# One of eight drive products of a selective scan moved from VectorE to GpSimd, and two TensorE steps put ahead of a sum

## The chip, the cores and the metric

The kernel is one program on one core of a Trainium2 chip. The metric is the device time of one execution in microseconds; three runs of the kernel before give a median of 766.16 us (764.79 to 766.89). PE is TensorE, DVE VectorE, ACT ScalarE, POOL GpSimd and SP SyncE.

## What is computed

A small fusion model runs over 16 sequences of 113 tokens (36 image patches and 77 text tokens) with 256 channels: patch embedding, attention, a mixture of experts, then a state-space layer and a quantised feed-forward layer. The change lies in the state-space layer. Cut to what matters, for one sequence:

```python
delta = softplus(rank @ dt_proj_w.T + dt_proj_b)             # token x channel
dA  = exp(delta[..., None] * A)                              # 16 states
dBu = delta[..., None] * Bp[:, :, None, :] * xc[..., None]
ys  = scan(h[t] = dA[t] * h[t-1] + dBu[t])
y   = (ys * Cp[:, :, None, :]).sum(-1) + xc * D_param
y   = y * silu(res)
return y @ out_proj_w.T + out_proj_b + (x @ skip_proj_w.T + skip_proj_b)
```

`Bp` and `Cp` depend on token and state, not on the channel. `delta * xc` (called `dx` in the kernel) depends on token and channel, not on the state. So the drive `dBu` of one state is `dx` times one row of B.

## The kernel before

Channels lie on the partitions (2 blocks of 128), tokens along the free axis. The 16 sequences make 8 groups of two, N = 226 tokens each. The 16 states make 8 chunks of two, so a tile of a chunk is 128 x 904: two states, two channel blocks, 226 tokens. Every engine runs its own program over groups and chunks, written out by hand (`step` in `pool_ssm`, `act_ssm`, `dve_ssm` and `pe_ssm`), and they meet by semaphores; groups 1 to 4 run in a hardware loop, two to a turn, the others are written out. Within a chunk c of a group g:

- PE, `spread` (L1832 to 1842): two products with a selection matrix copy the two rows of B to all 128 partitions, into PSUM bank 2 or 3 by the parity of c. It is issued one chunk ahead, at the head of PE's chunk c - 1, and waits until the drive that read the bank last is done.
- DVE, `drives` (L1327 to 1333): `dx` times the spread B from PSUM, into one of two drive buffers. One product of 128 x 904.
- ACT, `decays` (L821 to 829): exp(delta A) of each state into PSUM, one chunk ahead, each of the two after the scan that read that buffer last.
- DVE, `scans` (L1335 to 1342): two scans of 128 x 452, state = decay * state + drive.
- POOL (L501 to 522): `read`, the product of the states with C (128 x 904), after both scans of the chunk. In chunks 0, 1, 2, 3 and 7 (`PAIRED`) POOL then adds the two states, a pair sum of 128 x 452.
- PE, `reduce` (L1844 to 1862): adds `read`, or the pair sum, to the sum over the states in PSUM. It is issued in PE's next chunk, behind the spread.

Other work is put between these at fixed chunks, by constants. On DVE in chunk 1 `gate` (L1344), the product with silu(res) of the group before, and in chunk 2 `add_resid` (L1349), the residual and its statistics. On ACT the silus in chunk 1, `projections` (L796) in chunk 3, softplus in chunk 4. On POOL, at the head of chunk 3 `without_high` (L486), which waits for ACT's projections of the next group, of chunk 5 the two step products `steps` (L494), of chunk 6 `without_mid`. On PE, in the order of `step` (L1879): chunk 3 issues spread, reduce of chunk 2, `project_dt`, then the first half of `skip` (the skip projection of this group, L1864); chunk 4 issues spread, reduce of chunk 3, the second half of `skip`, and `turn`, which transposes the normalised rows of the group after the next; chunks 5 and 6 issue the two halves of `project_in` behind the reduce. Group 6 has no `turn` and no `project_in`, and in group 7 DVE also does the next layer's layernorm: statistics behind the scans of chunk 3, rows behind those of chunks 4 to 7.

The ordering of POOL's and DVE's chunks, in the kernel's own words:

```python
# pool_ssm.step, chunk c
pool.wait_ge(state_ready, 2 * k + 4)        # both scans of this chunk
pool.wait_ge(read_used, k + 1)
pool.tensor_tensor(read[kp], state[kp], c_all[...], ALU.mult)
if c in PAIRED:
    pool.tensor_tensor(read[kp][:, 0], read[kp][:, 0], read[kp][:, 1], ALU.add)
# dve_ssm.step, chunk c
drives(g, c, par)
if before and c == AT_GATE: gate(g - 1, 1 - par)
scans(g, c)
if before and c == AT_RESID: add_resid(g - 1)
```

Of the kernel before, what the change touches and what calls it, by code (L numbers as in the profile page):

```python
# [17 lines left out]
P = 128  # L18
# [38 lines left out]
AT_NORMALISE, AT_TURN, AT_COPY, AT_IN, AT_PAD, AT_CONV = 0, 4, 5, 5, 6, 7  # L57
OPENING = 1
AT_SKIP = (3, 4)
FILL = (19, 2, 4)  # L60
# [51 lines left out]
def build(nc, a, out):  # L112
    ctx = ExitStack()
    with ctx:
# [3 lines left out]
        def sem(name):  # L118
            return ctx.enter_context(nc.semaphore(name))
# [18 lines left out]
        work = sb("work", [P, WORK])  # L138
        ident = const[:, C_ID:C_ID + P]

        def psb(bank):
# [148 lines left out]
        read = [pl.take((2, KT, N)) for _ in range(2)]  # L290
        yT = pl.take((KT, N))


# [57 lines left out]
        xn2_ready, xn2T_ps, xT2_ready = sem("xn2_ready"), sem("xn2T_ps"), sem("xT2_ready")  # L351
        logitsT_ps, logitsT_ready = sem("logitsT_ps"), sem("logitsT_ready")
        logits_ps, route, chosen_ready, counts_ps, slots_ready = (sem("logits_ps"), sem("route"), sem("chosen_ready"),
# [15 lines left out]
        yT_ready, ssm_ps, resid3_ready = sem("yT_ready"), sem("ssm_ps"), sem("resid3_ready")  # L369
        pair_ready, decay_zero, shift_ready = sem("pair_ready"), sem("decay_zero"), sem("shift_ready")  # L370
        patch_in = [sem(f"patch_in{n}") for n in range(PK // 2)]
# [111 lines left out]
        def pool_ssm(pool):  # L483
# [10 lines left out]
            def steps(g, par):  # L494
# [4 lines left out]
                pool.tensor_tensor(dx[par], delta[par], xc[par], ALU.mult).then_inc(dx_ready, 1)  # L499

            def step(g, par, c_loads, more=True):  # L501
                for c in range(CHUNKS):
                    k = g * CHUNKS + c
                    kp = c % 2
                    if more and c == AT_REST:
                        without_high(g + 1)
                    if more and c == AT_STEPS:
                        steps(g + 1, 1 - par)
                    if more and c == AT_LOW:
                        pool.wait_ge(read_ready, k + 2)  # L510
                        without_mid(g + 1, 1 - par)
                        pool.wait_ge(bc3_ready, g + 2)
                    if c == 0:
                        pool.wait_ge(c_in[par], c_loads)
                    pool.wait_ge(state_ready, 2 * k + 4)
                    pool.wait_ge(read_used, k + 1)
                    pool.tensor_tensor(read[kp], state[kp], c_all[par][:, 2 * c:2 * c + 2, :].unsqueeze(2).broadcast_to([P, 2, KT, N]), ALU.mult)\  # L517
                        .then_inc(read_ready, 1)
                    if c in PAIRED:
                        pool.wait_ge(read_ready, k + 3)  # L520
                        pool.tensor_tensor(read[kp][:, 0], read[kp][:, 0], read[kp][:, 1], ALU.add).then_inc(pair_ready, 1)  # L521
# [127 lines left out]
        def act_shared(act):  # L649
            def gate(n, par):  # L650
                act.wait_ge(sgate_ps, n + par + 1)
                act.wait_ge(sh_ready, n + par + 1)
                act.activation(s_gate[:, par, :], ps[:, 3 + 2 * par, 0:4 * S], ACT.Silu).then_inc(sgate_ready, 1)  # L653

            for par in range(2):
                gate(0, par)
            act.wait_ge(logitsT_ps, 1)
            act.activation(logitsT, ps[:, 7, 0:4 * S], ACT.Copy).then_inc(logitsT_ready, 1)
            with act.Fori(1, (4 * HT) // 2) as i:
                for par in range(2):  # L660
                    gate(2 * i, par)
# [99 lines left out]
        def act_ssm(act):  # L761
# [47 lines left out]
            def softplus(g):  # L809
# [9 lines left out]
                act.activation(sp_abs, sp_abs, ACT.Ln, bias=1.0).then_inc(softplus_ready, 1)  # L819

            def decays(g, c, par, first=False):  # L821
                k = g * CHUNKS + c
# [8 lines left out]
            def step(g, par, more=True, before=True, turn_next=True):  # L831
                for c in range(CHUNKS):
# [9 lines left out]
                    if c < CHUNKS - 1:  # L842
                        decays(g, c + 1, par)
                    elif more:
                        decays(g + 1, 0, 1 - par)
                    if not before and c == OPENING:
                        pad(1)
# [20 lines left out]
            decays(0, 0, 0, first=True)  # L868
            act.wait_ge(shift_ready, 1)
            step(0, 0, before=False)  # L870
# [158 lines left out]
        def dve_router(dve):  # L1029

            dve.wait_ge(logits_ps, 1)
            q = Seq(dve, route)
# [263 lines left out]
        def dve_ssm(dve):  # L1296
# [11 lines left out]

            for counted in (state_ready, read_ready, read_used, drive_ready):
                dve.sem_inc(counted, 2)  # L1310
# [24 lines left out]
            def scans(g, c):  # L1335
                k, kp = g * CHUNKS + c, c % 2
                dve.wait_ge(drive_ready, k + 3)
                dve.wait_ge(read_ready, k + 1)
# [18 lines left out]
            def step(g, par, more=True, before=True, turn_next=True):  # L1357
                for c in range(CHUNKS):
                    drives(g, c, par)
                    if before and c == AT_GATE:  # L1360
# [18 lines left out]
            normalise(1)  # L1379
            dve.scalar_tensor_tensor(out=shift[:, :], in0=mean[:, :], scalar=-1.0, in1=rstd[:, :], op0=ALU.mult, op1=ALU.mult).then_inc(shift_ready, 1)  # L1380
            dve.wait_ge(wqT_ready, 2 + 2 * FT + FT // 2)
            for n in range(2):
                dve.memset(decay_ps(n)[:, :, 0:1], 0.0).then_inc(decay_zero, 1)
            dve.wait_ge(decay_zero, 2)
            opening_steps()
# [174 lines left out]
        def pe_scores(pe):  # L1560

            pe.wait_ge(xT2_ready, B)
            for k in range(KT):
                for g in range(4):
                    rows = slice(ROUTED * g, ROUTED * g + ROUTED)
                    last = pe.matmul(ps[rows, 7, 0:4 * S], router_w[:, k, :], xT2[:, k, g * 4 * S:(g + 1) * 4 * S], start=k == 0,
                                     stop=k == KT - 1, tile_position=(0, ROUTED * g), skip_group_check=True)
            last.then_inc(logitsT_ps, 1)

# [212 lines left out]
        def pe_ssm(pe):  # L1782
# [49 lines left out]

            def spread(g, c, par):

                k, kp = g * CHUNKS + c, c % 2
                if c == 0:
                    pe.wait_ge(bc3_ready, g + 1)
                    pe.wait_ge(proj_ready, 4 * g + 4)
                pe.wait_ge(drive_ready, k + 1)
                for n in range(2):  # L1840
# [38 lines left out]
            def step(g, par, more=True, before=True, turn_next=True):  # L1879
                for c in range(CHUNKS):  # L1880
                    if c < CHUNKS - 1:
                        spread(g, c + 1, par)
                    elif more:
                        spread(g + 1, 0, 1 - par)
# [8 lines left out]
                    if before and c == AT_OUT:  # L1893
                        project_out(g - 1)
                    if c > 0:
                        reduce(g, c - 1, par)
                    if more and c == AT_RANK:
                        project_x(g + 1, 1 - par)
                    if more and c == AT_DT:
                        project_dt(g + 1)  # L1900
                    if c in AT_SKIP:
                        if before:
                            pe.wait_ge(resid3_ready, g)
                        skip(g, par, AT_SKIP.index(c))
                    if turn_next:
                        if c == AT_TURN:
                            turn(g + 2)
                        if AT_IN <= c < AT_IN + 2:
                            project_in(g + 2, par, c - AT_IN)
                        if c == AT_CONV:  # L1910
                            convolve(g + 2, (0,))
# [15 lines left out]
            turn(1)  # L1927
            spread(0, 0, 0)
            step(0, 0, before=False)
# [106 lines left out]
```

## Time and profile before

| | |
|---|---|
| median of 3 runs | 766.16 us (764.79 to 766.89) |
| profiled execution | 768.96 us |
| its span, first to last instruction | 767.0 us |
| granted TensorE clock, mean | 0.965 of full speed |
| scan stage (first drive to last gate) | about 440 to 693 us |

The times of rows of the trace are counted from the start of the span. The chip's answer to a wait is read from the row behind it: in square brackets stands how long the engine idled before the row, and the line that released it.

### The profile page before, as it was taken

The page shows a single profiled execution, that of the slowest core. Times are in us where ns is not written, and L with a number is a line of the kernel's source. Part 1 is how long each engine was busy: PE and PEld are TensorE (multiplying, and loading weights), DVE is VectorE, ACT ScalarE, POOL GpSimd, SP SyncE. Part 2 cuts the span into 40 slices and gives each one's busy share as a digit, 9 for nine tenths or more (in the row PEclk, how much of TensorE's full clock was granted, in tenths as well). Part 3 has the DMA queues.
Part 4 walks back from the last instruction along what each step waited for, and adds up shares of the span by engine and source line. Part 5 has one row for each costly group of instructions (what it writes and reads, how often), then busy time and mean ns, then how long its engine had stood idle before and what let it go on. Part 6 is the DMA issues. An engine that isn't in the chain of part 4 may idle for free. (4 is left out here: it accounts for less than half of the span.)

```text
span 767.0 us, 11714 instructions
## 1 busy us (share of the span) xinstructions
PE 689.1 (90%) x3814; PEld 453.1 (59%) x3814; DVE 493.9 (64%) x895; ACT 375.6 (49%) x852; POOL 296.3 (39%) x249
## 2 busy tenths in 40 slices
PE   7789999998999999999996689899899897759986
PEld 5568888886566655666664556557566564324444
DVE  1466666666542215444215779998999899995686
ACT  0366666665311122233222666875876774212964
POOL 0011111110026013111211058888888888430436
PEclk9999999999999999999998899999999999978999
DMA  9990000001213041111004202202201201000003
GB/s 242 359 409 23 0 0 0 0 0 38 88 26 98 0 120 35 49 42 35 21 28 112 98 14 84 99 14 85 97 25 72 98 33 66 0 0 1 1 0 97
DMA packets 17831, 50.04 MB, mean 65 GB/s; under 512 B 3935, under 2 KB 12291, under 8 KB 15619
## 3 DMA queue, kind: packets, MB, share of 16 engines
q1 hardware_dynamic: 15683, 43.79, 16.6%
q0 software_dynamic: 2112, 5.77, 2.7%
q8 instruction: 22, 0.36, 0.2%
q14 instruction: 14, 0.11, 0.0%
HBM read 42.85 MB, written 6.70 MB: 65 GB/s over the span
## 5 line engine op out<-in xcount | busy, mean ns | idle before, releaser
L517 POOL TENSOR_TENSOR arena<-arena 128x904 f32<-128x904 f32 x64 | 125.0, 1953 | 43.6 <-DVE arena L1341 39.5
L1341 DVE TENSOR_TENSOR_SCAN arena<-ps,arena 128x452 f32<-128x452 f32 x128 | 133.6, 1086 | 6.9 <-ACT ps L828 2.1
L828 ACT ACTIVATE ps<-arena,sh_w 128x448 f32<-128x448 f32 x128 | 79.1, 631 | 71.8 <-DVE arena L1341 71.5
L1666 PE MATMUL ps<-arena,work 128*128 x176 | 84.2, 603 | 0.0
L592 ACT ACTIVATE work<-ps,work 113x113 f32<-113x113 f32 x256 | 66.8, 387 | 31.3 <-DVE work L960 31.3
L1331 DVE TENSOR_TENSOR arena<-arena,ps 128x904 f32<-128x904 f32 x64 | 69.2, 1081 | 11.6 <-PE ps L1841 11.3
L563 POOL DMA_INDIRECT answers_e<-work,slot_token x22 | 21.6, 980 | 135.1 <-DVE work L1131 132.3
L456 POOL TENSOR_TENSOR xT<-work 128x452 f32<-128x452 f32 x16 | 15.1, 943 | 141.2 <-DVE work L949 141.2
L1854 PE MATMUL ps<-arena,const 128*128 128x452 f32 x80 | 42.5, 615 | 19.1 <-POOL arena L521 18.7
L1859 PE MATMUL ps<-arena,const 128*128 128x452 f32 x96 | 44.7, 590 | 12.5 <-POOL arena L517 12.5
L1127 DVE TENSOR_TENSOR work<-ps,work 128x512 f32<-128x512 f32 x22 | 15.2, 692 | 55.8 <-PE ps L1666 50.1
L1615 PE MATMUL ps<-xT,sh_w 128*128 128x452 f32 x128 | 50.3, 545 | 0.0
L521 POOL TENSOR_TENSOR arena<-arena 128x452 f32<-128x452 f32 x40 | 45.7, 1143 | 3.1
L1678 PE MATMUL ps<-arena,work 128*128 x176 | 42.5, 384 | 3.5 <-ACT work L674 3.5
L1666 PEld LDWEIGHTS ps<-arena,work 128*128 128x128 f32 x176 | 31.5, 194 | 23.2 <-issue 22.6
L960 DVE TENSOR_REDUCE work<-ps 113x4 f32<-113x452 f32 x64 | 35.7, 621 | 10.6 <-PE ps L1469 10.6
L1678 PEld LDWEIGHTS ps<-arena,work 128*128 128x128 f32 x176 | 32.0, 192 | 7.9 <-issue 4.4
L1615 PEld LDWEIGHTS ps<-xT,sh_w 128*128 128x128 f32 x128 | 23.8, 190 | 21.7 <-issue 20.8
L653 ACT ACTIVATE work<-ps 128x452 f32<-128x452 f32 x16 | 8.7, 548 | 55.3 <-PE ps L1615 55.3
L1448 PE MATMUL ps<-work 128*128 128x113 f32 x256 | 33.2, 284 | 2.4 <-ACT work L586 1.7
L670 ACT ACTIVATE work<-ps 128x512 f32<-128x512 f32 x22 | 13.2, 598 | 45.0 <-PE ps L1666 45.0
L1475 PE MATMUL ps<-const,work 113*113 113x113 f32 x256 | 33.6, 264 | 1.7 <-ACT work L592 1.7
(270 smaller groups left out, 1385.5 us busy)
## 6 DMA issues: line engine op xcount, KB each, us to landing
arena<-c_rows SPq DMA_DIRECT2D x8, 1808.0 KB, 6.4
arena<-in_ex_w SPq DMA_DIRECT2D x8, 1536.0 KB, 21.6
rows_in<-xn SPq DMA_DIRECT2D x4, 448.0 KB
xn<-answers_e SPq DMA_DIRECT2D x4, 448.0 KB
out<-resid SPq DMA_DIRECT2D x8, 224.0 KB
arena<-in_patches SPq DMA_DIRECT2D x3, 576.0 KB, 6.3
sh_w<-in_sh_w SPq DMA_DIRECT2D x1, 1536.0 KB, 12.8
resid<-in_txt SPq DMA_DIRECT2D x1, 1232.0 KB
```

Source lines behind the costliest of these rows:

```text
L517: pool.tensor_tensor(read[kp], state[kp], c_all[par][:, 2 * c:2 * c + 2, :].unsqueeze(2).broadcast_to([P, 2, KT, N]), ALU.mult)\
L521: pool.tensor_tensor(read[kp][:, 0], read[kp][:, 0], read[kp][:, 1], ALU.add).then_inc(pair_ready, 1)
L592: last = act.activation(probs[:, r, j], ps[0:S, 3 + r, j * S:(j + 1) * S], ACT.Exp, bias=negmax[:, h:h + 1])
L828: act.activation(decay_ps(n)[:, :, 1:], delta[par].rearrange("p k (b s) -> p (k b) s", b=GB)[:, :, 1:], ACT.Exp, scale=a_neg[:, 2 * c + n: ...
L960: dve.tensor_reduce(negmax[:, 4 * r:4 * r + 4].unsqueeze(2), ps[0:S, 3 + r, 0:4 * S].rearrange("p (j s) -> p j s", j=4), AX.X, ALU.max, ne ...
L1331: dve.tensor_tensor(drive[kp], dx[par].unsqueeze(1).broadcast_to([P, 2, KT, N]), ps[:, 2 + kp, 0:2 * N].rearrange("p (n s) -> p n s", n=2) ...
L1341: dve.tensor_tensor_scan(state[kp][:, n].rearrange("p k s -> p (k s)"), decay_ps(n).rearrange("p q s -> p (q s)"), drive[kp][:, n].rearran ...
L1615: last = pe.matmul(ps[:, bank, 0:4 * S], sh_w[:, at + k * HID + m * P:at + k * HID + (m + 1) * P], xT2[:, k, bass.ds(g * 4 * S, 4 * S)], s ...
L1666: last = pe.matmul(ps[:, bank, :], xgT[par][:, k, :], arena[:, bass.ds(e * EW + at + k * HID, HID)], start=k == 0, stop=k == KT - 1)
L1678: last = pe.matmul(ps[:, 6, 0:D], e_hT[:, m, :], arena[:, bass.ds(e * EW + DOWN + m * D, D)], start=m == 0, stop=m == HT - 1)
L1854: pe.matmul(ps[:, 6, 0:KT * N], ident, read[kp][:, 0].rearrange("p k s -> p (k s)"), start=False, stop=c == CHUNKS - 1, skip_group_check=T ...
L1859: last = pe.matmul(ps[:, 6, 0:KT * N], ident, read[kp][:, n].rearrange("p k s -> p (k s)"), start=False, stop=False, skip_group_check=True)
```

## The change

In chunk 3 of every group, DVE makes no drive. ACT copies the spread B of that chunk from PSUM to a new tile of 128 x 452 in SBUF, `b_copy`, behind the decays of chunk 3. POOL multiplies `dx` by that copy into the drive buffer, at the head of its chunk 3: behind the product with C and the pair sum of chunk 2, ahead of `without_high`. DVE's scans of chunk 3 wait for that product, and so does PE's spread of chunk 5, which reuses the bank. On PE, the second half of `skip` and `turn`, both in chunk 4, are issued ahead of the reduce of chunk 3 instead of behind it. To have semaphores for this, some elsewhere are shared now: the router's two products use one (`logits_ps`), the zeroing of the decays and the shift of the layernorm another (`entry_ready`); `drive_ready` counts seven drives a group. The core of the diff:

```diff
+POOL_DRIVE = 3
+DVE_DRIVES = CHUNKS - 1
...
+        def dve_drives(g, c):
+            return DVE_DRIVES * g + c + 1 - (c > POOL_DRIVE)
...
+        b_copy = pl.take((2, N))
...
+            def drives(g, c, par):
+                k, kp = g * CHUNKS + c, c % 2
+                pool.wait_ge(b_copied, g + 1)
+                pool.wait_ge(dx_ready, g + 1)
+                pool.tensor_tensor(drive[kp], dx[par].unsqueeze(1).broadcast_to([P, 2, KT, N]),
+                                   b_copy.unsqueeze(2).broadcast_to([P, 2, KT, N]), ALU.mult).then_inc(pool_drive_ready, 1)
+
             def step(g, par, c_loads, more=True):
                 for c in range(CHUNKS):
                     k = g * CHUNKS + c
                     kp = c % 2
+                    if c == POOL_DRIVE:
+                        drives(g, c, par)
                     if more and c == AT_REST:
                         without_high(g + 1)
...
+            def copy_b(g, c):
+                act.wait_ge(b_ps, g * CHUNKS + c + 1)
+                if not isinstance(g, int) or g > 0:
+                    act.wait_ge(pool_drive_ready, g)
+                act.activation(b_copy, ps[:, 2 + c % 2, 0:2 * N].rearrange("p (n s) -> p n s", n=2), ACT.Copy).then_inc(b_copied, 1)
...
                         decays(g, c + 1, par)
                     elif more:
                         decays(g + 1, 0, 1 - par)
+                    if c + 1 == POOL_DRIVE:
+                        copy_b(g, c + 1)
...
-                dve.wait_ge(drive_ready, k + 3)
+                if c == POOL_DRIVE:
+                    dve.wait_ge(pool_drive_ready, g + 1)
+                else:
+                    dve.wait_ge(drive_ready, dve_drives(g, c))
...
-                    drives(g, c, par)
+                    if c != POOL_DRIVE:
+                        drives(g, c, par)
...
-                pe.wait_ge(drive_ready, k + 1)
+                if c == POOL_DRIVE + 2:
+                    pe.wait_ge(pool_drive_ready, g + 1)
+                elif c >= 2:
+                    pe.wait_ge(drive_ready, dve_drives(g, c - 2))
+                elif not first:
+                    pe.wait_ge(drive_ready, dve_drives(g - 1, CHUNKS + c - 2))
...
+                    if c == AT_SKIP[1]:
+                        skip(g, par, 1)
+                    if turn_next and c == AT_TURN:
+                        turn(g + 2)
                     if c > 0:
                         reduce(g, c - 1, par)
...
-                    if c in AT_SKIP:
+                    if c == AT_SKIP[0]:
                         if before:
                             pe.wait_ge(resid3_ready, g)
-                        skip(g, par, AT_SKIP.index(c))
+                        skip(g, par, 0)
                     if turn_next:
-                        if c == AT_TURN:
-                            turn(g + 2)
```

## Rows read from the trace of the kernel before

**Rows 1.** The page's costliest groups: count, busy us, mean ns, idle before and its releaser

```profile
L517 POOL TENSOR_TENSOR arena<-arena 128x904 f32<-128x904 f32 x64 | 125.0, 1953 | 43.6 <-DVE arena L1341 39.5
L1341 DVE TENSOR_TENSOR_SCAN arena<-ps,arena 128x452 f32<-128x452 f32 x128 | 133.6, 1086 | 6.9 <-ACT ps L828 2.1
```

**Rows 2.** Two of five stretches from gate to gate: us, then PE, PEld, DVE, ACT, POOL

```profile
504.02:533.53 29.51, 27.28 (x109) 17.84 (x108) 26.76 (x30) 20.93 (x41) 24.80 (x18) 0.94 0.17 64
533.53:561.77 28.24, 25.95 (x111) 17.22 (x110) 26.51 (x28) 20.48 (x40) 24.32 (x18) 1.00 0.16 66
```

**Rows 3.** Timeline of group 3, all engines: start us, us, row, idle before it

```profile
537.27 2.09 DVE L1341 TENSOR_TENSOR_SCAN arena<-ps,arena 128x452 f32<-128x452 f32 x2
...
539.43 1.96 POOL L517 TENSOR_TENSOR arena<-arena 128x904 f32<-128x904 f32 x1
...
540.75 1.08 DVE L1331 TENSOR_TENSOR arena<-arena,ps 128x904 f32<-128x904 f32 x1
540.92 1.19 ACT L828 ACTIVATE ps<-arena,sh_w 128x448 f32<-128x448 f32 x2
541.47 1.15 POOL L521 TENSOR_TENSOR arena<-arena 128x452 f32<-128x452 f32 x1
541.97 2.09 DVE L1341 TENSOR_TENSOR_SCAN arena<-ps,arena 128x452 f32<-128x452 f32 x2
...
542.52 0.45 ACT L800 ACTIVATE arena<-ps,sh_w 64x226 f32<-64x226 f32 x1 [0.41 <-PE ps L1823]
...
543.98 1.07 DVE L1331 TENSOR_TENSOR arena<-arena,ps 128x904 f32<-128x904 f32 x1
...
544.57 1.94 POOL L517 TENSOR_TENSOR arena<-arena 128x904 f32<-128x904 f32 x1
...
547.79 1.03 PE L1854 MATMUL ps<-arena,const 128*128 128x452 f32 x2 [0.85 <-POOL arena L521]
...
550.10 0.55 ACT L764 ACTIVATE arena<-ps 128x452 f32<-128x452 f32 x1 [0.57 <-PE ps L1793]
...
551.92 1.94 POOL L517 TENSOR_TENSOR arena<-arena 128x904 f32<-128x904 f32 x1
...
557.55 1.10 DVE L1331 TENSOR_TENSOR arena<-arena,ps 128x904 f32<-128x904 f32 x1 [0.66 <-PE ps L1841]
```

**Rows 4.** Timeline of DVE: three rows of group 2, the stall of group 6

```profile
507.76 2.09 DVE L1341 TENSOR_TENSOR_SCAN arena<-ps,arena 128x452 f32<-128x452 f32 x2
...
522.48 1.10 DVE L1331 TENSOR_TENSOR arena<-arena,ps 128x904 f32<-128x904 f32 x1 [1.51 <-PE ps L1841]
...
529.09 1.10 DVE L1331 TENSOR_TENSOR arena<-arena,ps 128x904 f32<-128x904 f32 x1
...
633.59 1.10 DVE L1331 TENSOR_TENSOR arena<-arena,ps 128x904 f32<-128x904 f32 x1 [1.13 <-PE ps L1841]
```

**Rows 5.** Timeline of PE, group 2, chunk 4: the sum and the skip product

```profile
518.29 1.55 PE L1854 MATMUL ps<-arena,const 128*128 128x452 f32 x2 [0.86 <-POOL arena L521]
519.63 1.91 PE L1868 MATMUL ps<-sh_w,arena 128*113 128x256 f32 x4
```

**Rows 6.** Stretches of 2 us, groups 2 and 3: columns as rows 2, then PE's clock

```profile
518.00:520.00 2.00, 1.71 (x3) 0.93 (x4) 1.87 (x3) 1.96 (x5) 2.00 (x2) 0.66 1.08 427
...
546.00:548.00 2.00, 1.15 (x7) 0.69 (x6) 2.00 (x3) 1.94 (x5) 1.92 (x3) 1.00 1.05 405
```

**Rows 7.** Timeline of group 0, chunk 3: decays, scans, product with C

```profile
455.38 1.19 ACT L828 ACTIVATE ps<-arena,sh_w 128x448 f32<-128x448 f32 x2
...
456.15 2.09 DVE L1341 TENSOR_TENSOR_SCAN arena<-ps,arena 128x452 f32<-128x452 f32 x2 [2.06 <-ACT ps L828]
...
458.56 1.95 POOL L517 TENSOR_TENSOR arena<-arena 128x904 f32<-128x904 f32 x1
```

**Rows 8.** Timeline of DVE in group 7: scans of chunks 2 and 3

```profile
651.03 2.09 DVE L1341 TENSOR_TENSOR_SCAN arena<-ps,arena 128x452 f32<-128x452 f32 x2
...
655.52 2.09 DVE L1341 TENSOR_TENSOR_SCAN arena<-ps,arena 128x452 f32<-128x452 f32 x2
```

More of the change, by code:

```diff
@@ L351, in build @@
         xn2_ready, xn2T_ps, xT2_ready = sem("xn2_ready"), sem("xn2T_ps"), sem("xT2_ready")
-        logitsT_ps, logitsT_ready = sem("logitsT_ps"), sem("logitsT_ready")
+        b_copied, logitsT_ready = sem("b_copied"), sem("logitsT_ready")
         logits_ps, route, chosen_ready, counts_ps, slots_ready = (sem("logits_ps"), sem("route"), sem("chosen_ready"),
@@ L369, in build @@
         yT_ready, ssm_ps, resid3_ready = sem("yT_ready"), sem("ssm_ps"), sem("resid3_ready")
-        pair_ready, decay_zero, shift_ready = sem("pair_ready"), sem("decay_zero"), sem("shift_ready")
+        pair_ready, entry_ready, pool_drive_ready = sem("pair_ready"), sem("entry_ready"), sem("pool_drive_ready")
         patch_in = [sem(f"patch_in{n}") for n in range(PK // 2)]
@@ L656, in act_shared @@
                 gate(0, par)
-            act.wait_ge(logitsT_ps, 1)
+            act.wait_ge(logits_ps, 1)
             act.activation(logitsT, ps[:, 7, 0:4 * S], ACT.Copy).then_inc(logitsT_ready, 1)
@@ L868, in act_ssm @@
             decays(0, 0, 0, first=True)
-            act.wait_ge(shift_ready, 1)
+            act.wait_ge(entry_ready, 1)
             step(0, 0, before=False)
@@ L1029, in dve_router @@
         def dve_router(dve):
-            dve.wait_ge(logits_ps, 1)
+            dve.wait_ge(logits_ps, 2)
             q = Seq(dve, route)
@@ L1307, in dve_ssm @@
             dve_layernorm(dve, 3, FIRST_SEQS)
-            for counted in (state_ready, read_ready, read_used, drive_ready):
+            for counted in (state_ready, read_ready, read_used):
                 dve.sem_inc(counted, 2)
@@ L1379, in dve_ssm @@
             normalise(1)
-            dve.scalar_tensor_tensor(out=shift[:, :], in0=mean[:, :], scalar=-1.0, in1=rstd[:, :], op0=ALU.mult, op1=ALU.mult).then_inc(shift_ready, 1)
+            dve.scalar_tensor_tensor(out=shift[:, :], in0=mean[:, :], scalar=-1.0, in1=rstd[:, :], op0=ALU.mult, op1=ALU.mult).then_inc(entry_ready, 1)
             dve.wait_ge(wqT_ready, 2 + 2 * FT + FT // 2)
             for n in range(2):
-                dve.memset(decay_ps(n)[:, :, 0:1], 0.0).then_inc(decay_zero, 1)
-            dve.wait_ge(decay_zero, 2)
+                dve.memset(decay_ps(n)[:, :, 0:1], 0.0).then_inc(entry_ready, 1)
+            dve.wait_ge(entry_ready, 3)
             opening_steps()
@@ L1567, in pe_scores @@
                                      stop=k == KT - 1, tile_position=(0, ROUTED * g), skip_group_check=True)
-            last.then_inc(logitsT_ps, 1)
+            last.then_inc(logits_ps, 1)
         def pe_turn_scores(pe):
@@ L1831, in project_dt, with spread @@
                 last.then_inc(dt_ps, 1)
-            def spread(g, c, par):
+            def spread(g, c, par, first=False):
                 k, kp = g * CHUNKS + c, c % 2
@@ L1881, in step @@
                     if c < CHUNKS - 1:
-                        spread(g, c + 1, par)
+                        spread(g, c + 1, par, not before)
                     elif more:
@@ L1927, in pe_ssm @@
             turn(1)
-            spread(0, 0, 0)
+            spread(0, 0, 0, True)
             step(0, 0, before=False)
```

## The prediction

> **What bounds the kernel now.** I read the page's costliest groups first: POOL's product with C (64 of 1953 ns) and DVE's scans (128 of 1086 ns) lead them [rows 1], and both lie in the scan stage, so shares over the whole span, which has other stages with other limits, say little. The stretches from gate to gate then give one group each: 29.51 us with 26.76 us of DVE and 24.80 us of POOL, then 28.24 us with 26.51 and 24.32 us [rows 2]; three more groups are like these. DVE is all but full, so its work per group looks like the thing to cut, but POOL has less than 4 us free, and each needs the other's result.
>
> The timeline of group 3, where nothing is disturbed, shows the order [rows 3]. Call T the end of the second scan of chunk 2: 537.27 + 2.09 = 539.36. POOL starts the product with C of chunk 2 at 539.43, right at T, and its pair sum at 541.47; both are behind the scans, never ahead of them. DVE spends T to T+1.4 on the residual and its statistics, makes the drive of chunk 3 at 540.75 and starts its scans at 541.97, T+2.6. The next drive follows at 543.98, so a chunk takes DVE 3.23 us. POOL starts its product of chunk 3 at 544.57, T+5.2, and of chunk 5 at 551.92; PE sums that product, projects and spreads, and only then can DVE start the next group's first drive, at 557.55 after 0.66 us of idling: T+18.2. So two chains, DVE's and POOL's into PE's, end within 0.7 us of each other.
>
> Groups 2 and 5 are longer because the drive of chunk 6 waits 1.51 us in both for its spread [rows 4]. PE was waiting for the pair sum of chunk 3, then did the sum in 1.55 us and the skip product behind it in 1.91 us [rows 5]; its granted clock was 0.66 in 518 to 520 us, falling to its lower level (1.2 GHz), while the same stretch of group 3 kept 1.00 (2.4 GHz) [rows 6].
>
> **The change part by part.**
>
> DVE loses one drive a group. Drive to first scan is 1.22 us (540.75 to 541.97) [rows 3]; eight groups give 9.8 us of DVE time back. That is the whole possible gain of this part, and it counts only where DVE isn't then waiting.
>
> ACT gains a copy of 128x452 from PSUM, behind the decays of chunk 3. The nearest row is the copy of the same size, 0.55 us; an upper bound is two of 0.45 us, 0.9 us [rows 3]; I take 0.55. The decays of chunk 3 end at 540.92 + 1.19 = 542.11 [rows 3], so the copy is there at about 542.66, T+3.3. What is queued behind it on ACT are the projections; they started at 542.52 after 0.41 us of waiting [rows 3], so they come some 0.2 us later; POOL's subtraction, which waits for them, stands behind the new product now and loses nothing.
>
> POOL gains a product of 128x904. It isn't in the trace. The product with C has the same shape, 1.95 us; from below, DVE's drive of 1.08 us, from above, two pair sums, each of half the size, at 1.15 us, 2.3 us [rows 3]. I take 1.95, by engine and shape. The Trainium skill (GPSIMD Engine Reference, section 3.1) measures the two-input product on this engine at 1.96 times DVE's; applied to 1.08 us that would be an estimate of 2.1 us and would add 0.15 us to each of eight groups.
>
> Its place matters more than its length. It stands at the head of POOL's chunk 3, behind chunk 2's product with C and pair sum. The pair sum ends at 541.47 + 1.15 = 542.62, T+3.26, the copy at T+3.3; the product runs to T+5.25 and, with 0.07 us to hand over (539.36 to 539.43), chunk 3's scans start at T+5.3 instead of T+2.6 [rows 3]. DVE is done with the residual at T+1.4, and the drive of chunk 4 is written behind those scans, so it idles 3.9 us there, pays 2.7 us for the 1.2 us it saves, and everything behind it moves by 2.7.
>
> From there both chains are followed to the next group's first drive. DVE: scans to T+7.3, then the drives of chunks 4 to 7 and 0, four steps of 3.23 us: T+20.2. POOL: chunk 3's product with C starts at T+7.45 instead of T+5.2, 2.25 us later; from there to chunk 5's product POOL took 7.35 us (544.57 to 551.92) [rows 3] and has the same to do, so that and PE's work behind it move by 2.25: T+20.45. The later one counts: **+2.25 us** an ordinary group, three of them (1, 3, 4). The 0.66 us stall is eaten by the shift.
>
> PE's skip product and turn ahead of the sum: PE has them done while it waits for the pair sum, and the spread of chunk 6 then follows the sum at once. In groups 2 and 5 the 1.51 us goes, but a DVE that arrives 2.7 us later wouldn't have met most of it: those groups reach their first drive at T+20.45 too. Group 2 did so at 529.09, with T = 507.76 + 2.09 = 509.85, T+19.24 [rows 4]: **+1.2 us** each. Alone, the reordering would be worth at most two times 1.51 us. In group 6 there is no in-projection of a coming group; DVE alone sets the pace, and the shift of 2.7 us eats its stall of 1.13 us [rows 4]: **+1.6 us**.
>
> Group 0 and group 7. In group 0 the decays of chunk 3 end at 455.38 + 1.19 = 456.57; with the copy, 457.1, and the product, 459.1, scans start at 459.2 instead of 456.15: 3.0; POOL's product with C starts at 461.35 instead of 458.56: **+2.8** [rows 7]. In group 7, T = 651.03 + 2.09 = 653.12, and scans start at T+5.3 = 658.4 instead of 655.52 [rows 8]: **+2.8**; DVE has layernorm work behind every later chunk there and nothing absorbs it.
>
> The shared semaphores cost nothing: the counts they wait for are reached at the same points as before.
>
> Sum: 3 x 2.25 + 2 x 1.2 + 1.6 + 2.8 + 2.8 = **16.4 us longer** (16.35). The profiled execution took 768.96 us and would take 785.4; the median of the runs is 766.16, 2.8 below it, and with 16.4 it is **782.6 us**.
>
> **The rivals.**
>
> A second loss, PE's clock. PE idles longer before the sum of chunk 3 and before those of 4 and 5. For it: the 0.85 us gap of group 3 and the 0.86 us gap of group 2 look alike, and the clock fell in one [rows 3, 5, 6]. Against it: low stretches sat in chunks 3 to 5, where the new order leaves slack. If the low level reaches the sum of chunk 5, in-projection and spread (551.92 + 1.94 = 553.86 to 557.55, 3.7 us [rows 3]) over half their length, each of the five groups 1 to 5 loses 1.8 us more: 9 us, about 791. The Trainium skill (TensorE: Matmul & The Clock Gate, Part 1) says idling drops the array to half rate; taken for every such gap, that would be this rival. The row of group 3 at 1.00 speaks against taking it for every gap.
>
> The reordering does not do what it says: if the sum itself at the low level, 1.55 us, still holds the spread of chunk 6, groups 2 and 5 keep their 1.5 us behind the new wait: +3 us, 785.6.
>
> The other side, faster: POOL makes the product before DVE asks for it. It decides at T+0.65: started by then, the product of 1.95 us ends by T+2.6, where the scans started before. Then groups 2, 5 lose their stalls, groups 0, 6 and 7 gain about 1.2 us each, and ordinary groups stay, for POOL's chain through chunk 5 sets them: 2 x 1 + 3 x 1.2 = 5.6 us less, 760.5. Against it: the written order puts a product and a pair sum, 3.1 us, between T and the start. Were it only half true, the result would be no change.
>
> **How the numbers follow.** Forecast 0.71, clock 0.14, reordering without effect 0.10, the other side 0.05, of which 0.03 faster and 0.02 within 0.3%, which is about 2.3 us and what a measurement of this kernel can tell from no change. So faster 0.03, same 0.02, slower 0.95. Range: from below, DVE's chain alone (T+20.2) in every ordinary group and 0.3 us less in each of the others, 2.5 us less in all, and a product 0.4 us quicker than its nearest row in eight groups, 3.2 us: 777. From above, the clock rival at 791, which also holds a product of 2.3 us (+2.8). The product at DVE's 1.08 us (0.87 us less, eight times) would take another 3.8 us off, 773, and is left out, as 64 rows of POOL say otherwise.
>
> **What would show it.** Right: DVE idle for some 3.9 us before the scans of chunk 3 in each group, released by a new POOL line of 8 products of about 1.95 us; 56 drives on DVE instead of 64; 8 ACT copies of about 0.55 us; gates 30.3 to 30.7 us apart; no wait of chunk 6's drive for its spread. Wrong: chunk 3's scans starting by T+3, a product well under 1.9 us, or gates still 28 us apart.

## The result, and the profile after

The changed kernel takes 786.16 us (median of 4 runs, 781.77 to 787.52), the kernel before 765.75 us in the same comparison: 1.0259 times as long, with a 95% interval of 1.0222 to 1.0296. The forecast was 782.6 us, with a range of 777 to 791. The profiled execution took 786.44 us, its span 784.5 us.

The costliest groups of the page, columns as in [rows 1], now put a wait in front of the scans that wasn't there. Lines have moved: in the changed kernel L1367 is the scans, L532 POOL's product with C, L536 its pair sum, L511 its new product, L840 ACT's copy, L1354 DVE's drives, L1873 PE's spread, L1886 and L1891 its sums of a pair sum and of a whole product, L1830 the in-projection.

```profile
L1367 DVE TENSOR_TENSOR_SCAN arena<-ps,arena 128x452 f32<-128x452 f32 x128 | 133.6, 1086 | 41.2 <-POOL arena L511 37.2
L532 POOL TENSOR_TENSOR arena<-arena 128x904 f32<-128x904 f32 x64 | 124.9, 1952 | 57.8 <-DVE arena L1367 52.5
...
L1354 DVE TENSOR_TENSOR arena<-arena,ps 128x904 f32<-128x904 f32 x56 | 60.4, 1078 | 6.8 <-PE ps L1873 6.6
```

The scans took 6.9 us of idling before, and 37.2 of the 41.2 us now end with L511, POOL's new product: 3.8 to 4.0 us in each of groups 1 to 7 and 9.5 in group 0, where DVE idled 3.4 us for the spread and 2.1 for the decays before. The instructions that were there take as long as before, a scan 1086 ns and the product with C 1952 (1953 before), so nothing in these rows says that the two engines slow each other. There are 56 drives on DVE instead of 64, as asked for, and POOL in its turn idles longer for the scans (52.5 us instead of 39.5). The view of the new line itself:

```profile
L511 POOL TENSOR_TENSOR arena<-arena x8: 1935/1937/1940, 452.8 to 670.0; 128x904 f32<-128x904 f32 x8
```

Least, median and greatest duration are the same to 5 ns: 1.94 us against the 1.95 forecast. Its place, in the timeline of group 3 (T, the end of chunk 2's second scan, is 542.53 + 2.09 = 544.62), beside [rows 3]:

```profile
542.53 2.09 DVE L1367 TENSOR_TENSOR_SCAN arena<-ps,arena 128x452 f32<-128x452 f32 x2
...
544.70 1.95 POOL L532 TENSOR_TENSOR arena<-arena 128x904 f32<-128x904 f32 x1
...
546.72 1.14 POOL L536 TENSOR_TENSOR arena<-arena 128x452 f32<-128x452 f32 x1
547.31 0.53 ACT L840 ACTIVATE arena<-ps 128x452 f32<-128x452 f32 x1
...
547.91 1.94 POOL L511 TENSOR_TENSOR arena<-arena 128x904 f32<-128x904 f32 x1
...
550.08 2.09 DVE L1367 TENSOR_TENSOR_SCAN arena<-ps,arena 128x452 f32<-128x452 f32 x2 [3.98 <-POOL arena L511]
...
552.25 1.94 POOL L532 TENSOR_TENSOR arena<-arena 128x904 f32<-128x904 f32 x1 [1.86 <-DVE arena L1367]
...
565.33 1.10 DVE L1354 TENSOR_TENSOR arena<-arena,ps 128x904 f32<-128x904 f32 x1 [0.33 <-PE ps L1873]
```

POOL's product with C, pair sum and new product stand one behind the other, ACT's copy ends at 547.84, just as the pair sum does (547.86), and DVE starts chunk 3 at T+5.46 after 3.98 us of idling. The next group's first drive comes at T+20.71. The forecast had T+5.3, 3.9 us and T+20.45.

By stretch, columns as in [rows 2], with PE's granted clock behind POOL's; the first runs from the first drive to the gate in group 1, the others from gate to gate:

```profile
435.85:475.02 39.17, 33.97 (x128) 23.21 (x127) 28.02 (x28) 23.79 (x46) 27.30 (x19) 0.88 0.15 61
475.02:508.04 33.02, 29.05 (x110) 18.74 (x109) 25.71 (x27) 21.59 (x42) 26.60 (x19) 0.90 0.15 58
508.04:538.79 30.75, 27.89 (x110) 18.07 (x109) 25.52 (x27) 21.20 (x41) 26.32 (x19) 0.94 0.16 61
538.79:569.55 30.76, 27.82 (x109) 18.02 (x109) 25.52 (x29) 21.41 (x41) 26.54 (x19) 0.94 0.15 61
569.55:600.25 30.70, 27.76 (x109) 18.00 (x108) 25.61 (x28) 21.55 (x41) 26.68 (x19) 0.94 0.16 61
600.25:630.69 30.44, 27.81 (x111) 18.11 (x110) 25.62 (x29) 20.89 (x40) 26.46 (x19) 0.94 0.16 62
630.69:661.10 30.41, 22.86 (x81) 12.32 (x80) 25.51 (x28) 19.08 (x35) 26.36 (x19) 0.94 0.17 62
661.10:709.04 47.94, 31.93 (x105) 14.44 (x104) 40.51 (x63) 8.63 (x15) 22.69 (x14) 0.88 0.00 0
```

Against the same stretches of the kernel before (first drive at 440.15, gates from 475.78 to 693.01) the scan stage is 273.19 instead of 252.86 us, 20.3 us longer. The span grew by 17.5 only: this execution reached its first drive 4.3 us earlier, and took 1.5 us longer behind the last gate. The profiles of the kernels below, which do the same work up to there, reach it between 435.4 and 439.7 us, and take 73.6 to 75.5 us behind the last gate (74.0 before), so neither is part of the change. DVE's work in a group fell by 1.0 us, and the group grew by 2.5.

Group 1, at 33.02 us, is longer than the rest. PE and DVE there:

```profile
491.69 1.03 PE L1886 MATMUL ps<-arena,const 128*128 128x452 f32 x2 [2.03 <-POOL arena L536]
...
493.68 3.38 PE L1891 MATMUL ps<-arena,const 128*128 128x452 f32 x4 [0.77 <-POOL arena L532]
496.85 3.17 PE L1830 MATMUL ps<-arena,sh_w 128*128 128x226 f32 x8
499.86 0.36 PE L1873 MATMUL ps<-arena,xT 96*128 96x226 bf16 x2
...
500.26 1.10 DVE L1354 TENSOR_TENSOR arena<-arena,ps 128x904 f32<-128x904 f32 x1 [2.25 <-PE ps L1873]
```

PE had its skip product and turn done and idled 2.03 us for the pair sum of chunk 3. Then the sum of chunk 4 took 3.38 us and the in-projection 3.17, where they take 1.79 and 1.69 in group 2, and chunk 7's drive waited 2.25 us for the spread behind them. The clock of the stretch, columns as in [rows 6]:

```profile
494.00:496.00 2.00, 2.00 (x3) 0.85 (x3) 1.87 (x3) 1.42 (x3) 1.92 (x3) 0.50 0.01 4
```

0.50 is the lower of the two levels, 1.2 GHz.

### The profile page after: what moved, and what is told of

It reads as the page before. It is cut to its first block and busy times, and to the rows that moved or that the text cites. A ratio compares the mean times of both kernels' runs of the same rounds, so it can differ in the third digit from the quotient of the medians.

```text
span 784.5 us, 11763 instructions
## 1 busy us (share of the span) xinstructions
PE 699.3 (89%) x3814; PEld 458.2 (58%) x3814; DVE 485.9 (62%) x887; ACT 380.8 (49%) x860; POOL 311.0 (40%) x257
## 5 line engine op out<-in xcount | busy, mean ns | idle before, releaser
L1367 DVE TENSOR_TENSOR_SCAN arena<-ps,arena 128x452 f32<-128x452 f32 x128 | 133.6, 1086 | 41.2 <-POOL arena L511 37.2
L532 POOL TENSOR_TENSOR arena<-arena 128x904 f32<-128x904 f32 x64 | 124.9, 1952 | 57.8 <-DVE arena L1367 52.5
L1693 PE MATMUL ps<-arena,work 128*128 x176 | 83.1, 596 | 0.0
L1891 PE MATMUL ps<-arena,const 128*128 128x452 f32 x96 | 49.8, 647 | 20.8 <-POOL arena L532 20.8
L1354 DVE TENSOR_TENSOR arena<-arena,ps 128x904 f32<-128x904 f32 x56 | 60.4, 1078 | 6.8 <-PE ps L1873 6.6
L1886 PE MATMUL ps<-arena,const 128*128 128x452 f32 x80 | 40.4, 587 | 19.4 <-POOL arena L536 18.8
L536 POOL TENSOR_TENSOR arena<-arena 128x452 f32<-128x452 f32 x40 | 45.7, 1143 | 3.1
L1705 PE MATMUL ps<-arena,work 128*128 x176 | 41.8, 380 | 3.4 <-ACT work L689 3.4
L1891 PEld LDWEIGHTS ps<-arena,const 128*128 128x128 f32 x96 | 18.7, 216 | 36.3 <-POOL arena L532 24.9
L1705 PEld LDWEIGHTS ps<-arena,work 128*128 128x128 f32 x176 | 31.8, 190 | 7.8 <-issue 4.4
```

Of the source, the lines that this page charges most:

```text
L1354: dve.tensor_tensor(drive[kp], dx[par].unsqueeze(1).broadcast_to([P, 2, KT, N]), ps[:, 2 + kp, 0:2 * N].rearrange("p (n s) -> p n s", n=2) ...
L1367: dve.tensor_tensor_scan(state[kp][:, n].rearrange("p k s -> p (k s)"), decay_ps(n).rearrange("p q s -> p (q s)"), drive[kp][:, n].rearran ...
L1693: last = pe.matmul(ps[:, bank, :], xgT[par][:, k, :], arena[:, bass.ds(e * EW + at + k * HID, HID)], start=k == 0, stop=k == KT - 1)
L1705: last = pe.matmul(ps[:, 6, 0:D], e_hT[:, m, :], arena[:, bass.ds(e * EW + DOWN + m * D, D)], start=m == 0, stop=m == HT - 1)
L1886: pe.matmul(ps[:, 6, 0:KT * N], ident, read[kp][:, 0].rearrange("p k s -> p (k s)"), start=False, stop=c == CHUNKS - 1, skip_group_check=T ...
L1891: last = pe.matmul(ps[:, 6, 0:KT * N], ident, read[kp][:, n].rearrange("p k s -> p (k s)"), start=False, stop=False, skip_group_check=True)
```

## The experiments

Times are medians; a ratio is to runs of the kernel before on the same chip (766.42, 765.44 and 766.10 us in the three comparisons), with its 95% interval. Stage is the time from the first drive to the last gate in the profiled execution: 252.86 us before, 273.19 us changed.

### The reordering alone

```diff
+                    if c == AT_SKIP[1]:
+                        skip(g, par, 1)
+                    if turn_next and c == AT_TURN:
+                        turn(g + 2)
                     if c > 0:
                         reduce(g, c - 1, par)
```

(in the kernel before; the same calls are taken out behind the sum)

> The kernel before with the reordering alone: PE issues the skip product's second half and the turn ahead of the sum of chunk 3; DVE still makes all eight drives. My theory: the reordering takes out the two waits of 1.51 us of chunk 6's drive (groups 2 and 5), and nothing else, so some 2 to 3 us under the kernel before: 763 to 764, with no wait of chunk 6's drive left in the trace. Rival (the reordering does nothing, since the clock falls all the same and the sum holds the spread): within 1 us of the kernel before, the 1.5 us waits still there. Rival (the reordering itself costs part of the loss of the change): slower than before by over 2.3 us.

762.84 us, 0.9966 times (0.9950 to 0.9982); stage 250.39. Groups 1 to 4 take 28.23, 28.24, 28.23 and 28.22 us, group 5 28.09, so the two of 29.5 and 29.1 us are gone, and with them the waits of 1.51 us. Group 2, columns as above:

```profile
500.69:528.93 28.24, 25.77 (x110) 16.97 (x109) 26.50 (x29) 20.68 (x40) 24.57 (x18) 1.00 0.17 67
```

The theory holds, and this kernel is faster than both, though only by 0.3% than the kernel before.

### The move alone

The changed kernel with those lines where they were before.

> The changed kernel with PE's order of before: only the drive of chunk 3 is moved to POOL. My theory: the move is the whole loss, 4 us of DVE waiting a group; the reordering matters less behind it than by itself. 786 to 789, DVE idle for 3.9 to 4.0 us before the scans of chunk 3 in each group. Rival (the reordering is part of the loss): under 784.

797.81 us, 1.0401 times (1.0377 to 1.0425); stage 281.51. The theory held for the wait (3.98 to 4.11 us in groups 1 to 7, 9.5 in group 0 as in the changed kernel) and missed the size, 9 us above its band: without the reordering the stage is 8.3 us longer than the changed kernel's (5.6 longer than in its second profile below), not up to 3. Group 1 shows why:

```profile
495.64 1.87 PE L1886 MATMUL ps<-arena,const 128*128 128x452 f32 x2 [3.29 <-POOL arena L536]
497.30 1.91 PE L1900 MATMUL ps<-sh_w,arena 128*113 128x256 f32 x4
```

PE now idles 3.29 us for the pair sum, then runs at the lower level (0.50 in 496 to 500 us) through the sum and the skip product, and chunk 6's spread stands behind both: DVE's drive waits 1.63 us for it. What happened to two groups in the kernel before now happens to all five that have a turn (31.8 to 33.0 us).

### Chunk 3 without a drive

Copy, product and their waits are taken out of the changed kernel; nothing replaces them.

> Nobody makes the drive of chunk 3: ACT's copy and POOL's product are left out, and the scans of chunk 3 read the drive buffer as chunk 1 left it, with no wait for POOL; PE's order is that of the change. It shows what DVE's time would have been worth at best. My theory: POOL's chain through chunk 5 into PE's spread sets the ordinary groups anyway, so of 9.8 us of DVE time only some 3 to 6 come through, with the 2 to 3 of the reordering: 757 to 763. Rival (DVE alone is the bound): the full 9.8 and the reordering, 753 to 755. Rival (the loss isn't in the wait, but in something else the change brings, such as the shared semaphores or code): 770 or more.

762.48 us, 0.9950 times (0.9934 to 0.9966); stage 248.46. At the upper end of the theory's band. Beside the reordering alone, DVE has eight drives less to make, and the groups are as long as there, for instance group 2:

```profile
501.90:530.17 28.27, 25.78 (x110) 16.97 (x109) 25.62 (x28) 20.70 (x40) 24.59 (x18) 1.00 0.18 67
```

28.27 us, with 25.62 us of DVE work instead of 26.50. Only group 7 is 2.0 us shorter. So of the 9.8 us of DVE time about 2 us come through: the best that the change could have given, had the product cost nothing. This kernel keeps the shared semaphores, so they are not the loss either.

### The product with nobody waiting for it

```diff
-                pool.tensor_tensor(drive[kp], dx[par]...
+                pool.tensor_tensor(unread, dx[par]...
```

(DVE doesn't wait for it; PE's spread of chunk 5 waits for the copy)

> As the kernel without a drive of chunk 3, but ACT makes the copy and POOL the product, at the place and of the size of the change; the product goes to a tile that nobody reads, and nobody waits for it but the copy's next turn (the scans of chunk 3 read the buffer as chunk 1 left it). It keeps the load on POOL and ACT and takes away DVE's wait. My theory: the load lies mostly in POOL's idle time ahead of chunk 3's product with C, and shifts that by some 0.6 us a group; 759 to 766, and the 20 us of the loss are the wait. Rival (POOL's load is the loss, 8 products of 1.95 us): 775 to 780.

767.86 us, 1.0019 times (1.0003 to 1.0036); stage 254.92. The theory's band ended at 766, so the load costs a little more than I held, 6.5 us of stage against no product at all, some 0.5 us an ordinary group (28.24 to 28.27 becomes 28.73 to 28.80) and 2.9 in group 7. Group 2:

```profile
500.78:529.54 28.76, 26.02 (x110) 16.99 (x109) 25.72 (x28) 21.12 (x41) 26.42 (x19) 1.00 0.17 66
```

The other 18.3 us (273.19 less 254.92) are DVE's wait and what follows from it, PE's clock included; against the kernel below in which the clock holds (269.34) they are 14.4.

### The product ahead of the pair sum

```diff
                         .then_inc(read_ready, 1)
+                    if c + 1 == POOL_DRIVE:
+                        drives(g, c + 1, par)
                     if c in PAIRED:
```

(and taken out at the head of chunk 3)

> The changed kernel with POOL's product one place earlier: behind the product with C of chunk 2, but ahead of its pair sum (1.1 us). Theory A: POOL's queue alone holds the product; it then starts at T+2.1 and DVE's wait shrinks from 4.0 to 2.9 us: 7 groups by 1.1, some 778 to 780 (less what the later pair sum takes back). Theory B, mine: ACT's copy comes at T+3.2 too, behind the silus and the decays of chunk 3, so the product can't start earlier; DVE's wait stays 3.9 to 4.0 us, POOL idles 1.1 us for the copy, and the pair sum comes 3 us later, which PE's sum and all behind it in chunk 3 pay: 786 to 792.

808.93 us, 1.0574 times (1.0542 to 1.0606). Theory B's steps are all there in group 1 (T = 482.84 + 2.09 = 484.93):

```profile
485.01 1.94 POOL L530 TENSOR_TENSOR arena<-arena 128x904 f32<-128x904 f32 x1
...
487.63 0.53 ACT L840 ACTIVATE arena<-ps 128x452 f32<-128x452 f32 x1
...
488.23 1.93 POOL L511 TENSOR_TENSOR arena<-arena 128x904 f32<-128x904 f32 x1 [1.27 <-ACT arena L840]
...
490.12 1.14 POOL L536 TENSOR_TENSOR arena<-arena 128x452 f32<-128x452 f32 x1
490.39 2.09 DVE L1367 TENSOR_TENSOR_SCAN arena<-ps,arena 128x452 f32<-128x452 f32 x2 [3.96 <-POOL arena L511]
...
491.31 1.87 PE L1886 MATMUL ps<-arena,const 128*128 128x452 f32 x2 [3.14 <-POOL arena L536]
...
499.35 1.10 DVE L1354 TENSOR_TENSOR arena<-arena,ps 128x904 f32<-128x904 f32 x1 [3.66 <-PE ps L1873]
```

The product can't start before the copy, DVE waits as long as ever, and the pair sum of chunk 2 comes 3 us late. What I had too small is what that costs: PE idles 3.14 us for it, does the sum, `project_dt` and the skip product at the lower level (0.50 from 492 to 501 us), and DVE waits another 3.66 us for the spread of chunk 5 behind them. Groups of 34.5 us, and 17 us above the top of the band.

### Chunk 4's drive instead, one place ahead

`POOL_DRIVE = 4`; ACT's copy stands behind the decays of chunk 3, POOL's product at the head of its chunk 3.

> The same move for chunk 4 instead of chunk 3, one place ahead: ACT copies the spread of chunk 4 behind the decays of chunk 3, POOL makes the product at the head of its chunk 3, ahead of the scans of chunk 3, DVE asks for it only behind those. Same load on every engine as in the changed kernel. My theory (the place is the loss, not the load): the product runs at T+4 to T+6, DVE asks for it at T+4.7 and waits some 1.3 us instead of 4.0; POOL's product with C of chunk 3 starts about 1.2 us late, so 766 to 774. Rival (the load of the product and the copy is the loss): within 4 us of the changed kernel, 782 to 790.

771.41 us, 1.0083 times (1.0054 to 1.0111); stage 257.46. Inside the theory's band, and 15.7 us of stage under the changed kernel with the same load on every engine (11.9 under the kernel below in which the clock holds, as it does here in groups 1 to 5). In group 2:

```profile
511.66 1.94 POOL L511 TENSOR_TENSOR arena<-arena 128x904 f32<-128x904 f32 x1 [0.66 <-ACT arena L840]
...
513.82 2.09 DVE L1367 TENSOR_TENSOR_SCAN arena<-ps,arena 128x452 f32<-128x452 f32 x2 [1.36 <-POOL arena L511]
```

The product runs beside chunk 3's scans, and DVE waits 1.36 us instead of 3.98. Most of the loss is the place. It still doesn't pay: 29.4 us a group.

### The product in halves

```diff
+                for n in range(2):
+                    pool.tensor_tensor(drive[kp][:, n], dx[par], b_copy[:, n]...).then_inc(pool_drive_ready, 1)
```

> The changed kernel with POOL's product made in two halves, one state each (128x452, as the pair sum, some 1.15 us), and each scan of chunk 3 waiting for its own half. My theory: the first scan starts 0.8 us earlier (T+4.65 instead of T+5.45), the second isn't held; POOL's total grows by 0.35 us but it then waits for the scans anyway. DVE's wait 3.2 us instead of 4.0, some 5 to 6 us less in all: 779 to 782. Rival (DVE's wait is not what sets the group; PE's chain does): no change, 785 to 788.

777.94 us, 1.0183 times (1.0138 to 1.0228); stage 266.02. Somewhat better than the band; the interval just meets the changed kernel's (1.0222 to 1.0296), so the traces have to carry the reading. In group 3 the two halves and the wait:

```profile
543.10 2.08 POOL L512 TENSOR_TENSOR arena<-arena 128x452 f32<-128x452 f32 x2
...
544.29 2.11 DVE L1368 TENSOR_TENSOR_SCAN arena<-ps,arena 128x452 f32<-128x452 f32 x2 [3.01 <-POOL arena L512]
```

The two take 2.08 us together, not 2.3, so the second scan isn't held, and the first starts 1 us earlier. Yet groups 2 to 4 are 30.72, 30.62 and 30.64 us, as in the changed kernel: there PE's sum of chunk 4 took 3.3 to 3.4 us, as in group 1 of the changed kernel, and DVE waited 0.9 us for the spread of chunk 7. In group 3:

```profile
551.69 3.38 PE L1892 MATMUL ps<-arena,const 128*128 128x452 f32 x4 [0.77 <-POOL arena L533]
...
556.90 1.10 DVE L1355 TENSOR_TENSOR arena<-arena,ps 128x904 f32<-128x904 f32 x1 [0.88 <-PE ps L1874]
```

The gain is in groups 0, 1, 6 and 7, and of the 3.2 us in group 1 some 2.3 are that its clock stayed at 1.00 here.

### The changed kernel once more

> The changed kernel itself, once more, to see which parts of its profile repeat. My theory: group 1, where PE's clock was at its lower level from 492 to 500 us and the first drive of group 2 waited 2.25 us, is chance; then that wait is 0.3 us as in groups 2 to 4, and the profiled execution is some 2 us shorter. Rival (the longer gap ahead of the sum throws the clock in group 1 every time): the 2.25 us wait is there again. 784 to 787 either way.

788.93 us (780.57 to 789.85), 1.0278 times (1.0211 to 1.0346); stage 275.93. The median is above the 784 to 787 of both theories. Neither held alone: the wait of 2 us is there again in group 1 (2.03 us, a group of 32.8) and now in group 3 too (2.21 us, 33.0); group 2 has 31.7 us with a wait of 0.90, and group 4 30.72. So group 1 repeats, groups 2 and 3 do not, and the profiled execution was 1.8 us longer, not shorter.

### PE kept at work ahead of the sum

```diff
-                for n in range(2):
+                for n in range(2) if c != POOL_DRIVE + 2 else (0, 1) * 5:
                     last = pe.matmul(ps[:, 2 + kp, n * N:(n + 1) * N], pick[...
```

> The changed kernel, in which PE makes the spread of chunk 5 five times over with the same result (eight more products of about 0.18 us, some 1.5 us), where it would otherwise idle 2.0 us ahead of the sum of chunk 3. It tests what the groups of 33 us are, which the profiles of the changed kernel show beside those of 30.7 (group 1 in one, groups 1 and 3 in the other). My theory: there PE idled 2.03 us ahead of the sum of chunk 3, its clock fell to the lower level for the sum of chunk 4 and the in-projection, and the spread of chunk 7 came 2.2 us late; with the idling filled, no group is over 31 us and the median is 781 to 785. Rival (the clock falls by the work of the stretch, not by that gap): groups of 33 us are there as before, 786 to 789. Rival (the added products delay the spread of chunk 5 and all behind it): every group 1 us or more longer, 790 or more.

782.88 us, 1.0229 times (1.0196 to 1.0261); stage 269.34. The stretches of groups 1 to 4:

```profile
475.35:506.09 30.74, 26.77 (x117) 17.65 (x116) 25.50 (x28) 21.41 (x41) 26.51 (x19) 1.00 0.16 62
506.09:536.84 30.75, 26.91 (x117) 17.77 (x117) 25.51 (x29) 21.42 (x41) 26.58 (x19) 1.00 0.16 61
536.84:567.58 30.74, 26.91 (x117) 17.78 (x117) 25.50 (x28) 21.40 (x41) 26.52 (x19) 1.00 0.15 61
567.58:598.30 30.72, 26.88 (x117) 17.76 (x117) 25.63 (x29) 21.57 (x41) 26.71 (x19) 1.00 0.16 61
```

The median is inside the theory's band. The clock stays at 1.00 in these stretches, and none of groups 1 to 6 is over 30.75 us. So the groups of 33 us are the clock, and the 30.74 us of the others is the wait alone. PE in group 1:

```profile
488.38 1.13 PE L1873 MATMUL ps<-arena,xT 96*128 96x226 bf16 x10
...
492.02 1.02 PE L1886 MATMUL ps<-arena,const 128*128 128x452 f32 x2 [1.26 <-POOL arena L536]
```

The added products lie where PE would have idled, which still leaves 1.26 of the 2.03 us, and cost DVE nothing. They are cheaper than I had put them: ten take 1.13 us and two 0.36, so the eight add 0.8 us, not 1.5.

### The next group's spread ahead of the in-projection

The reordering alone, with `spread(g + 1, 0, ...)` issued in chunk 6, ahead of `project_in`'s second half.

> The kernel before with the reordering alone, and one more step moved on PE: the spread of the next group's chunk 0 is issued ahead of the in-projection's second half instead of behind it. It tests whether the first drive's wait of 0.65 us, which stayed in every ordinary group when DVE had 1.2 us less to do, hangs on PE's queue. My theory: POOL's product of chunk 5, PE's sum, the in-projection and the spread are the chain that sets 28.24 us; with the in-projection out of it the wait goes, groups 1 to 5 come down to 27.6 us, 3 us in all: 759 to 761. Rival (another wait takes its place one chunk later, on POOL or on the second half of the in-projection): 762 to 764, as with the reordering alone.

763.53 us, 0.9966 times (0.9946 to 0.9986): the same as the reordering alone. The rival held:

```profile
553.98 1.07 DVE L1331 TENSOR_TENSOR arena<-arena,ps 128x904 f32<-128x904 f32 x1
...
557.90 1.10 DVE L1331 TENSOR_TENSOR arena<-arena,ps 128x904 f32<-128x904 f32 x1 [0.64 <-PE ps L1841]
```

The first drive of the group (553.98) no longer waits, and the second (557.90) waits 0.64 us instead, for its own spread, which PE issues behind the in-projection, the sum of chunk 6 and the convolution. Groups 1 to 4 take 28.21 to 28.23 us.

## Why the prediction was right

**The wait.** Right in place, cause and size: POOL's product starts at T+3.29, held by pair sum and copy at once, and DVE idles 3.98 us. It is shown by the kernel in which nobody waits (18.3 us of stage less) and by the one in which the same product stands elsewhere (15.7 us less); with the clock held it is 14.4 and 11.9. In group 0 the copy alone held the product, as forecast. One small term was off: the hand-over from POOL to DVE took 0.23 us (product's end at 549.85, scan at 550.08), where I had put 0.07 from the other direction [rows 3]. It makes 0.16 of the 0.25 us by which an ordinary group came out above 2.25; another 0.08 is POOL's way from chunk 3's product with C to chunk 5's, 7.43 us (552.25 to 559.68) where I had 7.35.

**The sum, group by group** (stretch after less stretch before, in us):

| group | 0 | 1 | 2 | 3 | 4 | 5 | 6 | 7 | all |
|---|---|---|---|---|---|---|---|---|---|
| forecast | 2.8 | 2.25 | 1.2 | 2.25 | 2.25 | 1.2 | 1.6 | 2.8 | 16.4 |
| changed | 3.54 | 4.78 | 1.24 | 2.52 | 2.48 | 1.33 | 2.12 | 2.32 | 20.3 |
| with PE kept at work | 2.73 | 2.50 | 1.24 | 2.50 | 2.50 | 1.32 | 1.77 | 1.92 | 16.5 |

With the clock held the working comes out to 0.1 us in the sum, in part by luck: the ordinary groups are 0.25 us long each and group 7 is 0.9 short. In group 7 something did absorb the shift, against the forecast: DVE's last gate idled 2.58 us for PE's sum before and 2.13 in the changed kernel. (The forecast's own figures give 2.9 there, 658.4 less 655.52, not 2.8.) Nor does DVE alone set group 6: the next group's first drive waits 0.67 us for its spread there, and without any drive of chunk 3 the group is as long (28.05) as with the reordering alone (28.13). The changed kernel's other 3.9 us are mostly the clock: 2.3 in group 1, 0.8 in group 0, where chunk 7's drive waits 1.13 us behind a sum of 3.21. Luck, too, is how close the profiled execution came, 786.44 us to 785.4: a stage 3.9 us longer than forecast and a first drive 4.3 us earlier nearly cancel. The median is 3.6 us above its forecast.

Taken in steps in this order, each the difference of two single profiles, the stage's 20.3 us are: the reordering 2.5 less, the drive left out 1.9 less, the load on POOL and ACT 6.5 more, the wait for the product 14.4 more, the clock 3.9 more.

**The clock.** I gave it as a rival with 0.14 and a price of 1.8 us in each of five groups. It came, beside the forecast, in one group of one profile and two of another, at 2.1 to 2.3 us each (under 1 us in group 0 of both and in group 2 of the second), and on the sum of chunk 4 with the first half of the in-projection, not on chunk 5's. The row on it is group 1's: 0.50 behind 2.03 us of idling. The Trainium skill (TensorE: Matmul & The Clock Gate, Part 1) says that idling lowers the clock; group 1 of this trace agrees with that. But the clock fell in group 2 as well, with no gap over 1 us ahead of it:

```profile
520.00:522.00 2.00, 2.00 (x6) 1.23 (x6) 2.00 (x3) 1.18 (x2) 0.50 (x1) 0.58 0.50 116
```

So the gap alone doesn't tell, and when the clock falls stays open. The argument against the rival was right in groups 2 to 4: the low stretch lies where the new order leaves slack, and they are as long (30.70 to 30.76 us) as with the clock held.

**The copy and the load.** ACT's copy took 0.53 us (0.55 forecast). I costed POOL's load at nothing beside the wait; alone it costs some 0.5 us an ordinary group and 2.9 in group 7, but behind the wait it adds nothing to an ordinary group, as POOL idles there (1.86 us ahead of chunk 3's product with C, at 552.25).

**The reordering.** Alone 2.5 us of stage, inside the 3 us at most that the forecast gave it. The step of the working that failed is the sentence that a later DVE "wouldn't have met most of it": with the move and without the reordering the stage is 8.3 us longer (281.51 less 273.19), for in every group with a turn PE now idles over 3 us ahead of the sum, the sum runs at the lower clock, and the spread of chunk 6 stands behind it. That the gap is what lowers the clock is not shown by itself.

**DVE's time.** That ordinary groups would keep their length even with the drive for free was right: 28.27 us without any drive. For the groups at the ends I had hoped for 3.6 us and the run shows 2.0. What exactly sets 28.2 us stays partly open: taking the in-projection out from ahead of the spread only moved the wait by one chunk.

## What to carry to other kernels

Before work goes from a full engine to one with room, look where in the other's queue it will stand and what it stands behind: here it stood behind two operations that can't start until the full engine is done, so that engine waited for 4 us to save 1.2. Ask also what the saved time is worth with the work simply left out; here it was 2 us in 766. And where two edits come together, time each alone: the one that pays (0.9966) was hidden in the other's loss.

## What the runs showed that I had not expected

The hand-over from POOL to DVE is not one number. It took 0.22 to 0.23 us in groups 1 to 4, which run in the hardware loop, and 0.03 to 0.04 in groups 0, 5, 6 and 7, which are written out. In group 5 the product ends at 611.31 and the scans follow at once:

```profile
609.37 1.94 POOL L511 TENSOR_TENSOR arena<-arena 128x904 f32<-128x904 f32 x1
...
611.35 2.09 DVE L1367 TENSOR_TENSOR_SCAN arena<-ps,arena 128x452 f32<-128x452 f32 x2 [4.00 <-POOL arena L511]
```

What the loop adds there was not traced. Two products of half the size took 2.08 us on POOL against 1.94 for the whole; a pair sum, which has the size of a half, reads 1.14. POOL's product took 1.80 times DVE's drive (1.937 to 1.078 us, DVE's with one operand in PSUM); the Trainium skill (GPSIMD Engine Reference, section 3.1) has 1.96, measured on an add of 2048 elements a partition, so here the measurement decides. And adding 0.8 us of useless products per group to PE made the scan stage shorter, 269.34 us where the changed kernel's two profiles have 273.19 and 275.93. The medians go the same way, 782.88 us against 786.16 and 788.93, but the intervals of their ratios overlap.
